# Column maxima of an attention kernel: from TensorE, VectorE and ScalarE to VectorE alone

## What is computed

```python
q = jnp.einsum('oc,bcn->bon', Wq, xf) + bq[None, :, None]
k = jnp.einsum('oc,bcn->bon', Wk, xf) + bk[None, :, None]
v = jnp.einsum('oc,bcn->bon', Wv, xf) + bv[None, :, None]
att = jnp.einsum('bdi,bdj->bij', q, k) / jnp.sqrt(jnp.asarray(d_k, x.dtype))
att = jax.nn.softmax(att, axis=-1)
out = jnp.einsum('bcj,bij->bci', v, att).reshape(b, c, h, w)
cat = jnp.concatenate([gamma * out, x], axis=1)
fused = jnp.einsum('oc,bchw->bohw', Wf, cat) + bf[None, :, None, None]
```

## Time and profile before

| | |
|---|---|
| runs of the kernel | 2033.51, 2033.55, 2033.58 us (median 2033.55) |
| the profiled execution | 2033.3 us, its span 2031.4 us |
| busy: TensorE / VectorE / ScalarE / GpSimd | 99% / 78% / 86% / 59% of the span |
| granted TensorE clock | 1.0 of full speed |

### The profile page before, as it was taken

The page is one execution under the profiler, slowest core; times in us unless marked ns, Lnnn a source line. Parts: engine busy times, 40 slices in busy tenths (PEclk is TensorE's granted clock), DMA queues, the critical chain, the costliest instruction groups (busy, mean ns, idle before and its releaser), DMA issues.

```text
span 2031.4 us, 45017 instructions
## 1 busy us (share of the span) xinstructions
PE 2015.3 (99%) x16232; PEld 1980.4 (97%) x16232; DVE 1584.9 (78%) x2157; ACT 1748.9 (86%) x2373; POOL 1206.1 (59%) x514
## 2 busy tenths in 40 slices
PE   9999999999999999999999999999999999999999
PEld 8999999999899999999989999999998999999999
DVE  6788888886778888888677888888867788888885
ACT  7888888887888888888788888888878888888886
POOL 0467766667056677666605666766660666677665
PEclk9999999999999999999999999999999999999999
DMA  4200000000310000000031000000003100000000
GB/s 136 84 22 22 15 15 21 21 21 12 120 70 22 22 21 15 16 21 21 11 125 65 22 21 21 21 10 21 21 11 130 38 22 21 21 21 18 13 21 17
DMA packets 54081, 69.46 MB, mean 34 GB/s; under 512 B 4048, under 2 KB 37584, under 8 KB 53968
## 3 DMA queue, kind: packets, MB, share of 16 engines
q1 hardware_dynamic: 53696, 67.91, 10.0%
q10 hardware_dynamic: 272, 0.07, 0.0%
HBM read 34.41 MB, written 33.55 MB: 33 GB/s over the span
## 4 chain that ended last, share of the span: by engine, by line
PE 92%; DVE 3%; ACT 3%; issue 2%; DMA 0%; DVEq 0%; ACTq 0%; SPq 0%
PE ps_o L388 72%; PE ps_s L380 11%; PE ps_p L242 3%; PE ps_o L242 2%; PE ps_t L284 1%; ACT queries L478 1%; ACT hi L453 1%; DVE val_lo L676 1%; PE ps_s L259 1%; PE ps_t L276 1%; PE ps_t L269 1%; DVE top L612 1%; DVE lo L599 1%; PE ps_t L242 0%; DVE raw L626 0%
## 5 line engine op out<-in xcount | busy, mean ns | idle before, releaser
L755 POOL TENSOR_TENSOR raw<-raw,top_m 128x1024 f32<-128x1024 f32 x508 | 1205.4, 2413 | 809.1 <-ACT top_m L464 809.1
L631 DVE TENSOR_TENSOR lo<-ps_p,hi 128x1024 fp32r<-128x1024 f32 x512 | 626.9, 1224 | 311.4 <-ACT ps_p L545 311.1
L612 DVE TENSOR_TENSOR top<-ps_s,top 128x512 f32<-128x512 f32 x960 | 660.0, 687 | 55.6 <-ACT raw L459 7.4
L538 ACT ACTIVATE hi<-raw 128x1024 fp32r<-128x1024 f32 x512 | 543.9, 1062 | 145.9 <-PE ps_o L388 141.4
L388 PE MATMUL ps_o<-val_hi,hi 128*128 128x258 f32 x4096 | 664.5, 284 | 4.1 <-ACT hi L538 4.1
L388 PE MATMUL ps_o<-val_lo,hi 128*128 128x256 f32 x4096 | 652.4, 281 | 0.0
L459 ACT ACTIVATE raw<-ps_s 128x512 f32<-128x512 f32 x1024 | 554.1, 595 | 54.7 <-PE ps_s L380 32.0
L388 PE MATMUL ps_o<-val_hi,lo 128*128 128x258 f32 x4096 | 599.3, 284 | 0.0
L388 PEld LDWEIGHTS ps_o<-val_hi,hi 128*128 128x128 f32 x4096 | 562.4, 189 | 5.8 <-issue 4.6
L388 PEld LDWEIGHTS ps_o<-val_lo,hi 128*128 128x128 f32 x4096 | 560.4, 189 | 0.0
L388 PEld LDWEIGHTS ps_o<-val_hi,lo 128*128 128x128 f32 x4096 | 538.7, 190 | 0.0
(11 more groups left out here) (72 smaller groups left out, 1028.3 us busy)
## 6 DMA issues: line engine op xcount, KB each, us to landing
xf<-x SPq DMA_DIRECT2D x32, 512.0 KB, 3.7
conv_d<-conv_st SPq DMA_DIRECT2D x64, 256.0 KB, 2.0
result<-conv_d SPq DMA_DIRECT2D x64, 256.0 KB, 2.6
out<-result SPq DMA_DIRECT2D x64, 256.0 KB, 2.2
raw<-wf2T SPq DMA_DIRECT2D x1, 256.0 KB, 3.9
raw<-wv SPq DMA_DIRECT2D x1, 256.0 KB, 4.3
raw<-wf1T SPq DMA_DIRECT2D x1, 256.0 KB, 4.7
raw<-wkqT ACTq DMA_DIRECT2D x1, 64.0 KB, 2.0
```

Of the source, the lines that this page charges most:

```text
L538: nc.scalar.activation(hi[:, t % 2], raw[:, slot].rearrange("p j i -> p (j i)"), ACT.Exp, scale=SCALE).then_inc(hi_done, 1)
L612: nc.vector.tensor_tensor(top[:, new], scores, top[:, new if half else old], ALU.max).then_inc(max_done, 1)
L631: nc.vector.tensor_tensor(lo[:, t % 2], ps_p[:].rearrange("p h n -> p (h n)"), hi[:, t % 2].bitcast(F32), ALU.subtract).then_inc(lo_done, 1)
L755: nc.gpsimd.tensor_tensor(raw[:, slot], raw[:, slot], top_m[:, r].unsqueeze(1).broadcast_to((P, JQ, I)), ALU.subtract).then_inc(sub_done, 1)
```

## The change

The maximum over the partitions is taken on VectorE alone. `top_j` is turned within squares of 32x32 (`turn_top`), so that each row of 32 along the free dimension holds 32 partitions of one query column; the largest of 32 is taken (`reduce_turned`, now from SBUF, 8 results per partition). Each of the four groups of 32 partitions now holds the maxima of its own 32 rows. The upper 64 partitions are copied to the lower ones and the larger taken, then the same with 32, and the result is copied back out to all four groups (`top_across`, six instructions, each waiting for the one before). Last it is turned back in 32x32 squares with each value repeated 32 times (`spread_top`), straight into `top_m`. Within a block, `top_j` and the turn stand in step 4, the reduction and `top_across` in step 5, and the turn back in step 6, ahead of that step's `lo` and folds. TensorE's four transposes and their waits are gone, and so is ScalarE's copy. TensorE's transposes of the output stay.

In the last chunk of a projection VectorE does all of it, with `subtract_first`, ahead of the values' `lo` parts; the convolution there writes `ps_t` in place of `ps_p`; and GpSimd waits for the end of `subtract_first` where it waited for the maxima. The hunk that declares the semaphores is left out, and so are blank lines.

```diff
--- before.py
+++ after.py
@@ -71,7 +71,13 @@
         top = sb("top", [P, 2, 2, I], F32)
         top_m = sb("top_m", [P, OUTS, I], F32)
         top_j = sb("top_j", [P, I], F32)
-        top_col = sb("top_col", [P, IT], F32)
+        top_turned = sb("top_turned", [P, I], F32)
+        top_group = sb("top_group", [P, I // 32], F32)
+        top_over = sb("top_over", [P // 2, I // 32], F32)
+        top_half = sb("top_half", [P // 2, I // 32], F32)
+        top_all = sb("top_all", [P, I // 32], F32)
         inv = sb("inv", [P, IT], F32)
         ident = sb("ident", [P, P], F32)
         wvf_hi = sb("wvf_hi", [P, KT, C_IN], F32R)
...
@@ -260,22 +267,6 @@
                                                 queries[:, bass.ds(n * I, I)], start=True, stop=True)
                     last.then_inc(s_ready, 1)
-            def turn_top(B, done):
-                if done is not None:
-                    pe.wait_ge(finished, done)
-                pe.wait_ge(top_j_done, B + 1)
-                for i in range(IT):
-                    last = nc.tensor.transpose(ps_t[:, i * P:(i + 1) * P], top_j[:, i * P:(i + 1) * P], ident[:])
-                last.then_inc(top_t_ready, 1)
-            def spread_top(B):
-                pe.wait_ge(top_col_done, B + 1)
-                for i in range(IT):
-                    last = nc.tensor.transpose(ps_t[:, I + i * P:I + (i + 1) * P], top_col[:, i:i + 1].broadcast_to((P, P)), ident[:])
-                last.then_inc(m_ready, 1)
             def turn_out(B):
                 pe.wait_ge(o_scaled, B * IT)
@@ -318,9 +309,9 @@
                     early_scores(c)
                     for j in range(JC):
                         project_values(j)
-                    turn_top(b * BLOCKS, None)
-                    pe.wait_ge(q_out, C + 1)
-                    convolve(ps_p[:, 0], 0, lambda: spread_top(b * BLOCKS))
+                    pe.wait_ge(conv_done, C * 2 - 1)
+                    convolve(ps_t[:], 0)
+                    pe.wait_ge(max_done, b * HALVES + 2 * len(MADE))
                     convolve(ps_s[:, LAST_CONV].rearrange("p j i -> p (j i)"), 1)
                     return
                 if start:
@@ -424,16 +415,11 @@
                     else:
                         lead(t, 1)
                         if t == 1 and not first:
-                            pe.wait_ge(m_done, B + 1)
                             turn_out(B)
-                        if t == 5 and not last_block:
-                            spread_top(B + 1)
                         scores_ahead(t)
                         pe.wait_ge(lo_done, Q + (t + 1))
                         trail(t, 0)
                         trail(t, 1)
-                        if t == 4 and not last_block:
-                            turn_top(B + 1, None if first else B)
             def finish_last(b):
                 turn_out(b * BLOCKS)
@@ -459,10 +445,6 @@
                     nc.scalar.activation(raw[:, slot, 2 * half:2 * half + 2], ps_s[:, (bank + half) % BANKS],
                                          ACT.Copy).then_inc(raw_done, 1)
-            def keep_top(B, r):
-                act.wait_ge(m_ready, B + 1)
-                nc.scalar.activation(top_m[:, r], ps_t[:, I:2 * I], ACT.Copy).then_inc(m_done, 1)
             def project(b, c, first):
                 C = snap(act, b * CHUNKS + c)
                 start = first and c == 0
@@ -498,8 +480,7 @@
                     conv_out(ps_p[:, 1], 1, C - 1)
                     values_out(0)
                     values_out(1)
-                    keep_top(b * BLOCKS, 0)
-                    conv_out(ps_p[:, 0], 0)
+                    conv_out(ps_t[:], 0)
                     act.wait_ge(sub0_done, b + 1)
                     exponential_hi(0, 0)
                     act.wait_ge(conv_done, C * 2 + 1)
@@ -562,8 +543,6 @@
                     elif not last_image:
                         act.wait_ge(pv_done, Q + t)
                         split_x(b + 1, 0)
-                    if t == 5 and not last_block:
-                        keep_top(B + 1, (r + 1) % OUTS)
                     if not (isinstance(n, int) and n * QUADS + t + AHEAD >= STEPS):
                         keep_scores(H, t + AHEAD, 2 * (QUADS * r + t + AHEAD) % BANKS, (QUADS * r + t) % SLOTS)
@@ -616,14 +595,39 @@
                 dve.wait_ge(max_done, folded)
                 nc.vector.tensor_tensor(top_j[:], top[:, 0, 0], top[:, 0, 1], ALU.max).then_inc(top_j_done, 1)
+            def turn_top(B):
+                dve.wait_ge(top_j_done, B + 1)
+                nc.vector.transpose(top_turned[:], top_j[:]).then_inc(top_t_done, 1)
             def reduce_turned(B):
-                dve.wait_ge(top_t_ready, B + 1)
-                nc.vector.tensor_reduce(top_col[:].unsqueeze(2), ps_t[:, 0:I].rearrange("p (i j) -> p i j", i=IT), AX_X,
-                                        ALU.max).then_inc(top_col_done, 1)
+                dve.wait_ge(top_t_done, B + 1)
+                nc.vector.tensor_reduce(top_group[:].unsqueeze(2), top_turned[:].rearrange("p (u k) -> p u k", k=32), AX_X,
+                                        ALU.max).then_inc(top_group_done, 1)
+            def top_across(B):
+                dve.wait_ge(top_group_done, B + 1)
+                nc.vector.tensor_copy(top_over[:], top_group[P // 2:P]).then_inc(half_over, 1)
+                dve.wait_ge(half_over, B + 1)
+                nc.vector.tensor_tensor(top_half[:], top_group[0:P // 2], top_over[:], ALU.max).then_inc(half_done, 1)
+                dve.wait_ge(half_done, B + 1)
+                nc.vector.tensor_copy(top_over[0:32], top_half[32:64]).then_inc(quarter_over, 1)
+                dve.wait_ge(quarter_over, B + 1)
+                nc.vector.tensor_tensor(top_all[0:32], top_half[0:32], top_over[0:32], ALU.max).then_inc(quarter_done, 1)
+                dve.wait_ge(quarter_done, B + 1)
+                nc.vector.tensor_copy(top_all[32:64], top_all[0:32]).then_inc(half_filled, 1)
+                dve.wait_ge(half_filled, B + 1)
+                nc.vector.tensor_copy(top_all[64:P], top_all[0:64]).then_inc(top_all_done, 1)
+            def spread_top(B, r):
+                dve.wait_ge(top_all_done, B + 1)
+                nc.vector.transpose(top_m[:, r], top_all[:].unsqueeze(2).broadcast_to((P, I // 32, 32))).then_inc(m_done, 1)
             def subtract_first(B):
                 dve.wait_ge(m_done, B + 1)
-                nc.vector.tensor_tensor(raw[:, 0], raw[:, 0], ps_t[:, I:2 * I].unsqueeze(1).broadcast_to((P, JQ, I)),
+                nc.vector.tensor_tensor(raw[:, 0], raw[:, 0], top_m[:, 0].unsqueeze(1).broadcast_to((P, JQ, I)),
                                         ALU.subtract).then_inc(sub0_done, 1)
             def split_p(Q, t):
@@ -682,10 +686,13 @@
                 if last_chunk:
                     early_scores(c)
                     reduce_top(b * HALVES + 2 * MADE[c] + 2)
+                    turn_top(b * BLOCKS)
+                    reduce_turned(b * BLOCKS)
+                    top_across(b * BLOCKS)
+                    spread_top(b * BLOCKS, 0)
+                    subtract_first(b * BLOCKS)
                     values_lo(0)
-                    reduce_turned(b * BLOCKS)
                     values_lo(1)
-                    subtract_first(b * BLOCKS)
                     split_p(b * STEPS, 0)
                     return
                 if start:
@@ -725,8 +732,12 @@
                         add_conv(B - 1, before, b * (16 * USES[before]) + (use * 16 + 16))
                     if t == 4 and not last_block:
                         reduce_top(H + 2 * 2 * QUADS)
+                        turn_top(B + 1)
                     if t == 5 and not last_block:
                         reduce_turned(B + 1)
+                        top_across(B + 1)
+                    if t == 6 and not last_block:
+                        spread_top(B + 1, (r + 1) % OUTS)
                     if t == QUADS - 1:
                         normalise(B, 0, first)
                     if t < QUADS - 1 or not last_block:
@@ -757,7 +768,7 @@
             def project(b, c, first):
                 if c == CHUNKS - 1:
-                    pool.wait_ge(m_done, b * BLOCKS + 1)
+                    pool.wait_ge(sub0_done, b + 1)
                     pool.sem_inc(sub_done, 1)
                     subtract_top(0, 1)
```

More of the change, by code:

```diff
@@ L117, in attention_conv @@
         s_ready, raw_done, max_done = sem("s_ready"), sem("raw_done"), sem("max_done")
-        top_j_done, top_t_ready, top_col_done = sem("top_j_done"), sem("top_t_ready"), sem("top_col_done")
-        m_ready = sem("m_ready")
+        top_j_done, top_t_done, top_group_done = sem("top_j_done"), sem("top_t_done"), sem("top_group_done")
+        half_over, half_done, quarter_over = sem("half_over"), sem("half_done"), sem("quarter_over")
+        quarter_done, half_filled, top_all_done = sem("quarter_done"), sem("half_filled"), sem("top_all_done")
         m_done, sub0_done = sem("m_done"), sem("sub0_done")
```

## The result

The changed kernel takes 2089.3 us (median of 4 runs, 2088.7 to 2089.6) against 2033.6 us before: a ratio of 1.0274, 95% interval 1.0261 to 1.0287, so it is 55.7 us slower. The forecast was 2074 in a range of 2040 to 2110.

A forecast was written before the change was run, and what follows sets the result against it. The prediction took TensorE, busy 99% of the span, as the bound. It summed -28.2 (transposes) + 56 x 1.2 (step 0 waits) + 1.7 (attention starts) = +40.7 us on 2033.3, giving 2074 us, range 2040 to 2110.

The forecast's parts named there:

- The mechanism: Steady block: maxima 3.1 us later delay GpSimd, ScalarE's exponentials and VectorE's fold, so TensorE waits for its bank in step 0.
- The price of VectorE's new instructions: VectorE, per block: turns 0.42 us each, copies 0.15, maxima 0.165; the six small ones in a row 1.11 us.
- cheap instructions: Rival: VectorE's small instructions are cheap and the wait shrinks or vanishes, down to 2007 us; chance 0.18, of which faster 0.12.
- two passes: Rival: each VectorE turn costs 0.69 us, the step 0 wait is 1.74 us, total 2104 us; chance 0.13.
- VectorE as the bound everywhere: Rival: every block is bound by VectorE with waits of its own, some 2 us each, total 2125 us; chance 0.07.
- the 2035: Estimate in us from the skill's 58 + columns cycles: cheaper VectorE instructions, 0.7 us less path, 0.5 us wait a block.
- TensorE's gain: Steps 4 and 5 without the transposes: 0.47 us a block off TensorE's queue, 28.2 us over 60 blocks.
- The wait: TensorE in step 0 waits 1.2 us for VectorE's fold to free the bank, in 56 blocks.
- 40.7: Forecast net loss in us: -28.2 + 56 x 1.2 + 1.7.
- Block 14: Last block preparing maxima in each image: no scores made ahead from step 4 on, so no bank wait: 0.
- The starts of attention: After each projection TensorE starts 0.43 us later, 4 times, 1.7 us in all.
- The rival on the other side: Rival: small instructions cheap or path to the subtraction 1.2 us shorter, no wait, 2007 us; chance 0.18, of which faster 0.12.

The follow-up runs named there:

- e1: Changed kernel with VectorE's turn back into top_m moved from step 6 to step 5, right behind the six small instructions; 2009.3 us, ratio 0.9880.
- e2: Kernel before, with only ScalarE's copy of the maxima to top_m moved from step 5 to step 6; 2104.7 us, ratio 1.0348.
- e5: e1 plus one more full-size GpSimd subtraction into an unread tile, after its wait for a block's maxima; 2086.2 us, ratio 1.0255.
- e7: Changed kernel with VectorE's fold of the first half of step 7's scores ahead of lo of the next block's step 0; 2110.4 us, ratio 1.0373.
- e4: Changed kernel with everything from the maximum to the turn back in step 4, ahead of its lo and folds; 2069.4 us, ratio 1.0175.
- e3: Changed kernel without the six small instructions, so each group of 32 partitions keeps its own maxima; 2032.7 us, ratio 0.9994.
- e6: Blocks 1 to 15 as in e1, block 0's maxima by TensorE and ScalarE as in the kernel before; 2005.7 us, ratio 0.9860.

## Why the prediction was right, and by how much it was off

**The mechanism** is the one that it named, link by link: turn back queued behind lo and the folds, GpSimd's first result, ScalarE's exponentials (ready 3.1 us late by the prediction, 3.19 by 9.49 - 6.30), VectorE's fold, TensorE's bank in step 0, 56 times. e1 takes the first link away, e2 makes the maxima late without the added work, e5 makes GpSimd's first result late though the maxima are early, e7 shows what stands behind the last.

**The price of VectorE's new instructions** was right: the turns take 0.445 and 0.435 us (0.42 taken), the six small ones 0.154 to 0.168 us (0.15 and 0.165 taken), 1.16 us in a row (1.11). The groups of two of them, in the changed kernel:

```profile
L601 DVE STREAM_TRANSPOSE top_turned<-top_j 128x256 f32<-128x256 f32 x64 | 28.5, 445 | 2.2
...
L613 DVE TENSOR_TENSOR top_half<-top_group,top_over 64x8 f32<-64x8 f32 x64 | 10.1, 158 | 2.2
```

That ends the rivals of cheap instructions and of two passes. The third, VectorE as the bound everywhere, is out too: in the changed kernel's block VectorE itself waits for ScalarE ahead of lo of steps 2 to 4 (0.89, 0.57 and 0.74 us), and all 56 waits of TensorE stand at the scores. By these rows the 58 + columns cycles of the Trainium skill (VectorE: DVE Perf Modes, The TRN2 errata) are too few for such instructions, by 0.09 us each, and the 2035 worked out from them falls too; the measurement decides. The fixed term of about 150 cycles that the same section gives as measured would make 0.165 us for 8 columns, an estimate, and the rows agree with it. The turn agrees with the Trainium skill (Vector Engine (DVE) Microarchitecture Reference, The reshape front-end and per-opcode configuration), which has it sustain one element a cycle per lane: a maximum of the same shape takes 0.431 us.

**TensorE's gain** was 0.47 a block; it measures 13.91 - 13.46 = 0.45 from step 4's start to step 0's (214.28 - 200.37, and 218.48 - 205.02).

**The wait was mis-sized**, and that is the larger part of the 15 us between 40.7 and 55.7. Said: 1.2 us. Measured: the second half of the scores starts at 220.92, due at 219.42 + 0.24, so 1.26 us late, and the next products follow after 0.34 us where 0.24 is usual, another 0.10. The prediction had no term for starting again, and it named the turns' duration as the first thing to read if the size was off, which explains only 0.04. Per block that is 1.36 - 0.45 = 0.91 for the 0.73 forecast. By the blocks' lengths it is 0.927: 52 of them took 48.2 us longer. 56 x 0.20 = 11 us.

**Block 14** was put at a gain of 0.47; it gains 0.16 (TensorE's turns of the output are 25.17 us apart there, where they were 25.33), for ScalarE waits 1.25 us for GpSimd there too: 1 us in all.

**The starts of attention** were put at 1.7 us together. The profiled execution is 56.1 us longer than before; without the blocks (56 x 0.927 = 51.9, less the 0.7 that block 14 gains) 4.9 are left for the starts. In two of the four something came on top that no step of the prediction had, a fall of TensorE's clock, 1.6 us each (last section). The other 1.7 match the forecast sum, but not start by start: in the first image TensorE starts at 76.56 where it was 75.89, 0.11 of which it had lost already in the projection, so 0.56 for the 0.43 forecast. What it waits for there is the exponential, as forecast, though the list of waits names VectorE's `val_lo` (changed kernel; then ScalarE before):

```profile
74.10 1.23 DVE L630 TENSOR_TENSOR raw<-raw,top_m 128x1024 f32<-128x1024 f32 x1
75.24 1.28 DVE L680 TENSOR_TENSOR val_lo<-ps_o,val_hi 128x512 fp32r<-128x512 f32 x2
75.36 1.06 ACT L519 ACTIVATE hi<-raw 128x1024 fp32r<-128x1024 f32 x1 [1.29 <-DVE raw L630]
```

```profile
74.70 1.06 ACT L538 ACTIVATE hi<-raw 128x1024 fp32r<-128x1024 f32 x1 [0.28 <-DVE raw L626]
```

The second `val_lo` ends at 76.52, but the code waits at this place only for the first, which is done by about 75.9, and for hi, which ends at 76.42, 0.14 us ahead of TensorE's start; before, it was 0.13 (75.76 and 75.89).

So 11 + 1 + 3 is the 15 that were missing, all of it on one side.

**The rival on the other side** (faster, if the path were 1.2 us shorter) was right in its condition, and e1 meets it by order, not by cheaper instructions: 2009, where 2007 was worked out for no wait at all.

## What to carry to other kernels

Moving work from the full engine to one with a fifth of its time free can lose, if what it makes feeds a chain over several engines: look for the first consumer in order (here an engine that is idle for 42% of the span), count what stands in front of the new instruction in its queue, and follow the lateness until it meets the full engine. The amount of added work mattered less than its place: same instructions, 2089 or 2009 us by the place of one. Of the places tried, neither the latest nor the earliest was best, but the work in two portions, each ahead of whatever wasn't due yet.

## What the runs showed of the hardware

**TensorE's clock after the start of attention.** In the changed kernel TensorE stands for 1.8 us there (0.7 to 1.3 before). In two of the four images its granted clock then falls to half, 1.2 in place of 2.4 GHz. Windows of the third image (stretch, busy time of TensorE, weight loads, VectorE, ScalarE, GpSimd, granted clock, share and rate of the DMA):

```profile
1111.00:1112.00 1.00, 0.00 (x0) 0.00 (x0) 1.00 (x2) 1.00 (x2) 0.96 (x1) 1.00 0.36 125
1112.00:1113.00 1.00, 0.92 (x6) 0.93 (x7) 0.16 (x2) 1.00 (x2) 1.00 (x1) 0.86 0.03 8
1113.00:1114.00 1.00, 1.00 (x7) 1.00 (x6) 1.00 (x1) 0.48 (x2) 1.00 (x2) 0.50 0.02 8
...
1115.00:1116.00 1.00, 1.00 (x6) 1.00 (x6) 0.01 (x1) 1.00 (x3) 1.00 (x2) 0.50 0.45 129
1116.00:1117.00 1.00, 1.00 (x10) 1.00 (x9) 1.00 (x1) 0.96 (x2) 1.00 (x1) 0.93 0.95 332
```

Groups of four products start 0.85 us apart there in place of 0.48, and step 0 takes 5.0 us (1112.08 to 1117.07) in place of 3.44. In the profiled executions, the kernels with this stand (1.7 to 1.8 us; the changed one, e1, e4, e5, e7) show the fall at 6 of 20 starts, those with a shorter one (0.5 to 1.6 us; the kernel before, e2, e3, e6) at none of 16. The single wait of 1.1 us in step 0 brought it on in none of the 56 blocks of the changed kernel; in e7, where TensorE stops twice there (0.6 us each), one of the 56 blocks had it. Why one start has it and the next doesn't is open, and so is whether the length of the stand decides; no run was made for it.

**A wait costs more than its length.** At the first stop of each block looked at, TensorE's next two products took about 0.10 us longer than their usual 0.24 us (220.92 to 221.26 here, the same 0.34 in e2 to e5). At 56 stops this is 6 us.
